# Projecting all keys and values in the prologue of a two-layer gated cross-attention kernel, with its loads and small steps put in another order

## The chip, the cores and the metric

The kernel runs on one core of a Trainium2 chip. The metric is device time in microseconds (us), the median of several executions. A separate profiled execution supplies the trace; its engines are PE (TensorE matmul), PEld (TensorE weight load), DVE (VectorE), ACT (ScalarE), POOL (GpSimd) and SP (SyncE, which here issues most transfers).

## What is computed

Two layers over x of 16 batches x 128 tokens x 256 channels. `ctx` has the same shape. Layer 0 is a WKV scan over `ctx` and a gated FFN; layer 1 is a cross-attention in which the 128 token positions are the channels (16 heads of 8), and a mixture of experts:

```python
x = x + tanh(g_xattn[0]) * wkv(time_decay, time_first, layernorm(x), ctx)      # scan along the tokens
x = x + tanh(g_ffn[0])   * ffn(layernorm(x))                                    # 256 -> 704 -> 256
# cross-attention, for each batch; target = layernorm(x), source = ctx
q = einsum('oc,bct->bot', Wq, target) + bq[None, :, None]
k = einsum('oc,bcs->bos', Wk, source) + bk[None, :, None]
v = einsum('oc,bcs->bos', Wv, source) + bv[None, :, None]
dot = einsum('bhdt,bhds->bhts', q, k) / sqrt(HEAD_DIM)
dot = mask * dot - (1.0 - mask) * NEG
out = einsum('bhts,bhds->bhdt', softmax(dot) * mask, v)
x = x + tanh(g_xattn[1]) * out
x = x + tanh(g_ffn[1]) * moe(layernorm(x))                                      # 8 experts of 256 tokens, 1 shared
```

The keys and values depend on `ctx`, `Wk`, `Wv`, `bk` and `bv` alone, not on x.

## The kernel before

Batches are taken in four groups (NG) of four (GB). The program has three blocks, one after the other. At the end of a block every engine waits for all the others, SP too.

**Block 1, the prologue (L497 to L759)**, holds WKV for all groups and the FFN for groups 0 to 2. SP issues the loads: x of group 0, the mask, `ctx` of group 0 into the one buffer `CV`, 15 small vectors (all counted on `s_ld`), the FFN weights (`s_wts`), then the next `ctx` once PE has read the last (`s_vT`), the other x, and the late weights. WKV of a group and half goes: PE turns the normalised x and `CV` (`pe_wkv_in`), ACT takes exponents (`act_exps`), DVE multiplies and scans (`dve_products`, `dve_scans`), POOL adds (`pool_sums`), DVE takes a reciprocal (`dve_recip`), POOL multiplies (`pool_quot`, writes Y), PE turns Y back (`pe_wkv_out`) and DVE adds it to X (`dve_x1`). After `dve_ln2` and `pe_z2T` comes the FFN of the group: six slices i, each with a gate and an up product on PE (`pe_gu`), a tanh on ACT, two steps on DVE (`dve_h1`, `dve_h`); slice i+2 reuses the banks of slice i and waits for its `dve_h`. `pe_down` follows. While group g is in the FFN, WKV of group g+1 runs in between, at places written by hand (`pe_group`, `dve_group`, `act_group`, `pool_group`).

In this block DVE also makes the mask rows `mparts` from `mrow` (L684 to L696 and three calls of `mask_part`, at L698, L716 and L720); the last call adds to `s_mp`. SP waits for `s_mp` at L547, issues 14 transfers of mask rows to the scratch tensor `stack_scr` in HBM (L567; 16 batches x 2 sides x 192 rows of 512 B, 3.1 MB), and waits at L569 until all have landed.

**Block 2, attention (L1224 to L1492)**. For each batch PE projects q from `Z3` and k from `CX` (`pe_proj_q`, `pe_proj_k`), ACT adds biases into `QK` (`act_qk`), POOL applies the mask (`pool_masked`), ACT and POOL split into bf16 parts, SP stores these to `stack_scr` and reads the stacked rows, with the mask rows, back into `QKA`. PE makes scores, DVE takes maxima (`dve_reduce`, 16 for each batch), PE makes turned scores, ACT takes exponents, PE multiplies with the values `VP`. Values: `pe_v` from `CX`, `dve_vf` adds the bias into `VF`, POOL writes `VP`. The order is a hand-written table of 8 slots p for each batch (`turns`). The block opens with the FFN of group 3, with the first projections and scores in between.

**Block 3, the experts (L1582 to the end)**, is not touched.

The engines do what is queued on them strictly in program order, so a wait holds all that stands behind it on that engine.

Of the kernel before, what the change touches and what calls it, by code (L numbers as in the profile page):

```python
# [50 lines left out]
def flamingo_kernel(nc, x, ctx, mask, g_xattn, g_ffn, time_decay, time_first, gate_wT, up_wT, down_wT,  # L51
# [10 lines left out]
    with ExitStack() as keep:  # L62
# [123 lines left out]
        with ExitStack() as part:  # L186
# [21 lines left out]
            CV = sbw("CV", [P, GB, C])  # L208
# [36 lines left out]
            s_c = semp("s_c")  # L245
# [5 lines left out]
            s_mT2 = semp("s_mT2")  # L251
            s_mask = semp("s_mask")
# [7 lines left out]
            s_xr = semp("s_xr")  # L260
            s_var2 = semp("s_var2")
# [22 lines left out]
            WB = [bank[4], bank[5]]  # L284
# [4 lines left out]
            def pe_wkv_in(pe, g, h):  # L289
# [4 lines left out]
                pe.wait_ge(s_exp, 2 * n)  # L294
# [3 lines left out]
                if h == 0:  # L298
                    pe.wait_ge(s_c, 16 * (g + 1))
                pe.wait_ge(s_pab, 2 * n)  # L300
                for b in range(GB):
                    last = pe.transpose(WB[1][:, b * P:(b + 1) * P], CV[:, b, h * P:(h + 1) * P], ident[:])
                last.then_inc(s_vT, 1)

            def act_exps(act, g, h):
# [6 lines left out]
            def dve_products(dve, g, h):  # L312
# [36 lines left out]
            def pe_wkv_out(pe, g):  # L349
# [9 lines left out]
            def dve_x1(dve, g):  # L359
# [11 lines left out]
            def dve_stats1(dve, ch, g):  # L371
                if isinstance(g, int) and g == 0:
                    dve.wait_ge(s_x, 16)
                else:
                    dve.wait_ge(s_xr, 16 * (NG - 1))
# [120 lines left out]
            N_SMALL, N_ROWS = 15, 14  # L496
            with nc.Block() as block:  # L497
                @block.sync
                def _(sp):
# [6 lines left out]
                    def load_ctx(g):  # L506
                        sp.dma_start(CV[:, :, :], ct[:, bass.ds(GB * g, GB), :]).then_inc(s_c, 16)

                    small = [(gates[:, 0:2], g_xattn.partition_broadcast(P)), (gates[:, 2:4], g_ffn.partition_broadcast(P)),
                             (td[:], time_decay), (tf[:], time_first),  # L510
                             (gs[:, 0:NI - 1], gate_s[0:(NI - 1) * P].rearrange("(i p) -> p i", p=P)),
                             (us[:, 0:NI - 1], up_s[0:(NI - 1) * P].rearrange("(i p) -> p i", p=P)),
                             *[(dst[HALF_I * f:HALF_I * (f + 1), NI - 1:NI], src[(NI - 1) * P:INTER].rearrange("(p a) -> p a", a=1))
                               for dst, src in ((gs, gate_s), (us, up_s)) for f in range(2)],
                             (dsb[:], down_s.partition_broadcast(P)), (bvb[:], bv.partition_broadcast(P)),
                             (bqk[:, 0:1], bq), (bqk[:, 1:2], bk), (wq[:], wqT)]
                    assert len(small) == N_SMALL
                    with nc.allow_non_contiguous_dma(reason="small vectors"):
                        load_x(0)
                        sp.dma_start(mrow[:], mask).then_inc(s_mask, 16)  # L520
                        load_ctx(0)
                        for dst, src in small:
                            sp.dma_start(dst, src).then_inc(s_ld, 16)
# [6 lines left out]
                    sp.wait_ge(s_vT, 1 + 2)  # L530
                    load_ctx(1)
                    for g in range(1, NG):
                        load_x(g, s_xr)
                    sp.wait_ge(s_pool0, 10)
                    for dst, src in ((wk[:], wkT), (wv[:], wvT),
                                     (wgt[:, :, 0:NE], Wg.rearrange("(h p) e -> p h e", p=P)),
# [5 lines left out]
                    with sp.Fori(2, NG) as g:  # L542
                        sp.wait_ge(s_vT, 1 + 2 * g)
                        load_ctx(g)
# [221 lines left out]
            with ExitStack() as att:  # L766
# [228 lines left out]
                def dve_vf(dve, b):  # L995
                    dve.wait_ge(a_vps, b + 1)
                    if later(b):
                        dve.wait_ge(a_vp, b)
# [999 lines left out]
```

## Time and profile before

| | us |
|---|---|
| median of 3 runs | 587.51 (583.6, 587.51, 588.49) |
| the profiled execution | 581.58 |
| its span, first to last instruction | 579.8 |
| block 1 | 0 to 149.2 |
| in it, the first FFN product of group 0 | 43.3 |
| block 2 | 149.2 to about 434 |
| block 3 | about 434 to 579.8 |

Busy shares of the span: PE 84%, DVE 69%, PEld 46%, ACT 42%, POOL 38%. The mean granted TensorE clock is 0.978 of full speed. HBM reads are 39.01 MB, writes 22.43 MB. A share is a mean over stages with different limits, so the stages are read one by one: who is idle, and what released it.

### The profile page before, as it was taken

How to read it: one execution, taken by the hardware profiler on the slowest of the kernel's cores; microseconds unless marked ns; L12 is line 12 of the kernel's file. 1: busy time of each engine (PE TensorE's matmuls, PEld its weight loads, DVE VectorE, ACT ScalarE, POOL GpSimd, SP SyncE). 2: the span in 40 equal slices, each digit the busy share in tenths (PEclk: the TensorE clock that was granted, in tenths of full speed). 3: DMA queues.
4: the chain of work that ended last, by engine and by line, in shares of the span. 5: the costliest groups of instructions: out<-in, count | busy, mean ns of one | idle time of the engine just before them, and what ended most of it. 6: DMA issues, size and time to landing. Idle time of an engine off the chain costs nothing. (4 is left out here: it accounts for less than half of the span.)

```text
span 579.8 us, 10728 instructions
## 1 busy us (share of the span) xinstructions
PE 487.7 (84%) x3400; PEld 269.2 (46%) x3400; DVE 397.8 (69%) x871; ACT 243.7 (42%) x478; POOL 217.8 (38%) x353
## 2 busy tenths in 40 slices
PE   1149999999696769899988888888779999899994
PEld 1034564747353424333343343333233555578883
DVE  4989879695336778888888888887755733333331
ACT  1132233121231048777777777777741001123331
POOL 2526234231283235555555555531301370024334
PEclk9999999999997969999999999999899999999998
DMA  5901007630267054655555555450004024157873
GB/s 139 334 2 36 1 6 119 88 43 0 73 179 191 20 135 131 154 157 145 140 154 144 144 145 144 125 128 5 5 2 149 32 105 138 55 126 194 195 151 36
DMA packets 68246, 61.94 MB, mean 107 GB/s; under 512 B 8992, under 2 KB 63248, under 8 KB 68208
## 3 DMA queue, kind: packets, MB, share of 16 engines
q1 hardware_dynamic: 65136, 57.25, 37.8%
q0 software_dynamic: 3072, 4.21, 4.3%
q8 instruction: 20, 0.33, 0.2%
q14 instruction: 18, 0.15, 0.1%
HBM read 39.01 MB, written 22.43 MB: 106 GB/s over the span
## 5 line engine op out<-in xcount | busy, mean ns | idle before, releaser
L1008 DVE TENSOR_REDUCE MX<-psum 128x2 f32<-128x512 f32 x256 | 166.3, 681 | 31.6 <-PE psum L874 31.5
L1086 ACT ACTIVATE HP<-psum 128x512 f32<-128x512 f32 x256 | 138.6, 600 | 43.6 <-PE psum L880 42.9
L874 PE MATMUL psum<-QKA 60*128 60x256 bf16 x512 | 82.0, 279 | 18.3 <-DVE MX L1008 16.7
L880 PE MATMUL psum<-QKA 60*128 60x256 bf16 x512 | 80.0, 277 | 9.4 <-ACT HP L1086 7.4
L953 PE MATMUL psum<-HP,VP 128*32 128x256 f32 x1024 | 82.9, 397 | 0.2 <-ACT HP L1086 0.2
L437 PE MATMUL psum<-space_a,space_w 128*128 128x512 f32 x160 | 72.8, 606 | 4.1 <-PEq L497 2.4
L874 PEld LDWEIGHTS psum<-QKA 60*128 60x128 bf16 x512 | 35.3, 95 | 64.9 <-DVE MX L1008 47.8
L1656 POOL DMA_INDIRECT out_x<-OE,to_u x16 | 25.0, 1562 | 72.6 <-ACT OE L1697 70.2
L437 PEld LDWEIGHTS psum<-space_a,space_w 128*128 128x128 f32 x160 | 29.8, 193 | 40.4 <-issue 34.4
L1795 PE MATMUL psum<-XT,WE 128*128 128x256 f32 (+1 forms) x192 | 44.1, 380 | 1.6 <-ACT XT L1681 1.6
L1721 PE MATMUL psum<-space_a,wsh 128*128 (+3 forms) x96 | 42.8, 595 | 0.8 <-PEq L1224 0.8
L880 PEld LDWEIGHTS psum<-QKA 60*128 60x128 bf16 x512 | 33.2, 95 | 20.7 <-ACT HP L1086 14.8
L478 PE MATMUL psum<-space_w,HP 128*128 128x256 f32 x160 | 41.2, 404 | 1.7 <-DVE HP L464 1.7
L1795 PEld LDWEIGHTS psum<-XT,WE 128*128 128x128 f32 (+1 forms) x192 | 34.2, 181 | 8.2 <-issue 1.1
L450 ACT ACTIVATE space_a<-psum,hgs 128x512 f32<-128x512 f32 (+1 forms) x24 | 15.5, 647 | 49.7 <-PE psum L437 38.8
L1116 POOL TENSOR_TENSOR VP<-VF,maskT 128x32 f32<-128x32 f32 x128 | 25.9, 239 | 26.9 <-DVE VF L999 15.8
L478 PEld LDWEIGHTS psum<-space_w,HP 128*128 128x128 f32 x160 | 30.2, 198 | 9.0 <-issue 5.5
L1098 POOL TENSOR_TENSOR QK<-QK,MB 128x512 f32<-128x512 f32 x16 | 20.3, 1269 | 36.0 <-ACT QK L1059 36.0
L953 PEld LDWEIGHTS psum<-HP,VP 128*32 128x32 f32 x1024 | 20.6, 109 | 26.9 <-issue 16.6
L1949 DVE SCALAR_TENSOR_TENSOR H1s<-THs,psum 128x256 f32<-128x256 f32 (+1 forms) x24 | 10.1, 420 | 31.5 <-ACT THs L1688 31.5
L334 POOL TENSOR_TENSOR DEN<-SB,EB 128x512 f32<-128x512 f32 x8 | 18.6, 2327 | 34.3 <-DVE SB L324 34.3
L1666 ACT ACTIVATE THs<-psum 128x512 f32<-128x512 f32 (+1 forms) x12 | 7.1, 595 | 55.0 <-PE psum L1721 55.0
(183 smaller groups left out, 739.8 us busy)
## 6 DMA issues: line engine op xcount, KB each, us to landing
QKA<-stack_scr SPq DMA_DIRECT2D x32, 480.0 KB, 5.4
stack_scr<-PARTS SPq DMA_DIRECT2D x32, 192.0 KB, 2.1
WE<-in_W SPq DMA_DIRECT2D x16, 352.0 KB, 4.0
stack_scr<-PARTS SPq DMA_DIRECT2D x32, 128.0 KB, 1.9
XD<-dispatched SPq DMA_DIRECT2D x8, 258.0 KB, 3.7
X<-in_x SPq DMA_DIRECT2D x4, 512.0 KB, 5.5
CV<-in_ctx SPq DMA_DIRECT2D x4, 512.0 KB, 3.6
CX<-in_ctx SPq DMA_DIRECT2D x16, 128.0 KB, 5.1
```

Of the source, the lines that this page charges most:

```text
L437: last = pe.matmul(to[:, :], w[:, h, i * P:(i + 1) * P], ZT[:, h, :], start=(h == 0), stop=(h == 1))
L478: pe.matmul(to[f], HP[:, i, t * P:(t + 1) * P], dw[:, i, :], start=(i == 0), stop=False)
L874: return pe.matmul(to[:, tt * T:(tt + 1) * T], QKA[rows, k, 0, h, tt * P:(tt + 1) * P], QKA[rows, k, 1, h, :], start=True, stop=True)
L880: return pe.matmul(to[:, (j % 2) * T:(j % 2 + 1) * T], QKA[rows, k, 1, h, st * P:(st + 1) * P], QKA[rows, k, 0, h, :], start=True, stop=True)
L953: last = pe.matmul(PVB[32 * j:32 * j + 32, grp * T:(grp + 1) * T], VP[:, k, st, 4 * j + i, :], PT[:, i % 2, st, j, :], start=(i in (0, 3) ...
L1008: dve.tensor_reduce(MX[:, par, head_of(n), :], src[:, :].rearrange("p (a s) -> p a s", a=2), axis=AX.X, op=ALU.max).then_inc(a_red, 1)
L1086: act.activation(PT[:, i % 2, st, 2 * half:2 * half + 2, :].rearrange("p j t -> p (j t)"), TBK3[THIRDS[m]], ACT.Exp).then_inc(a_exp, 1)
L1098: pool.tensor_tensor(QK2, QK2, MB[:, k, :].unsqueeze(1).broadcast_to([P, 2, T]), ALU.mult).then_inc(a_masked, 1)
L1116: last = pool.tensor_tensor(dst, src, maskT[:, st, bass.ds(b, 1)].unsqueeze(2) .broadcast_to([P, 4, 8]), ALU.mult)
L1656: pool.indirect_dma_start(out=out_rows, out_offset=bass.IndirectOffsetOnAxis(ap=to_u[:, e, a:a + 1], axis=0), in_=OE[:, s, a, :], in_offse ...
L1721: last = pe.matmul(bank[2 * i + side][0:m, :], (wsh1, wsh3)[side][:, h, i * P:i * P + m], ZT4[:, h, bass.ds(GT * g, GT)], start=(h == 0), ...
L1795: last = pe.matmul(bank[i][0:m, lo:lo + CAP], w[:, s, h, i * P:i * P + m], XT[:, s, h, :], start=(h == 0), stop=(h == 1))
```

## The change

All of `ctx` is loaded once, in block 1, into `CTX` (16 batches), and stays there for the block. PE projects keys and values of all 16 batches in 16 units (`pe_keys_values`: a unit is two batches' keys or two batches' values), 12 before `pe_wkv_out` of group 0 and 4 after; ACT copies them to `KR` (with the key bias) and `VR`, which live through block 2. In block 2 `pe_proj_k`, `pe_v`, `dve_vf`, the key half of `act_qk` and the `CX` loads are gone; POOL masks keys and queries in two steps and adds the value bias itself in `pool_vp`.

Block 1 is put in another order as well: five small vectors are loaded from ACT's queue and have a semaphore of their own (`s_chain`); the ten other small ones are issued behind the FFN weights; the multiplication of `dw` by `dsb` goes from DVE to POOL; group 0's second half uses two further banks (`WB2`); `dve_recip(g + 1, 0)` stands behind slice 0 instead of ahead of it; the making of the mask rows goes from the start of the block to the DVE work of the last group.

```diff
+            def pe_keys_values(pe, u):
+                j, side = divmod(u, 2)
+                if u == 0:
+                    pe.wait_ge(s_wkv, 32)
+                if side == 0 and j % 2 == 0:
+                    pe.wait_ge(s_c[j // 2], 16)
+                if u == 1:
+                    pe.wait_ge(s_mT2, 1)
+                if u >= 2:
+                    pe.wait_ge(s_keep, u - 1)
+                if side == 0:
+                    last = pe.matmul(KV[0][:, :], wk[:], CTX[:, 2 * j:2 * j + 2, :].rearrange("p b t -> p (b t)"),
+                                     start=True, stop=True)
+                else:
+                    for b in range(2):
+                        for st in range(2):
+                            last = pe.matmul(KV[1][:, (2 * b + st) * P:(2 * b + st + 1) * P],
+                                             CTX[:, 2 * j + b, st * P:(st + 1) * P], wv[:], start=True, stop=True)
+                last.then_inc(s_pr, 1)
...
                     for h in range(2):
                         pool_sums(pool, 0, h)
+                    pool.wait_ge(s_wts, 80)
+                    pool.wait_ge(s_ld, 16 * N_SMALL)
+                    pool.tensor_tensor(dw[:, :, :], dw[:, :, :], dsb[:, :].unsqueeze(1).broadcast_to([P, NI, C]),
+                                       ALU.mult).then_inc(s_dw, 1)
                     for h in range(2):
                         pool_quot(pool, 0, h)
...
-                    with pe.Fori(0, NG - 2) as g:
-                        pe_group(g, False)
-                    pe_group(NG - 2, True)
+                    for g in range(NG - 1):
+                        pe_group(g, g == NG - 2)
...
                     def dve_group(ch, g, last):
-                        dve_recip(dve, g + 1, 0)
                         for i in range(NI):
                             dve_h1(dve, ch, g, i)
                             dve_h(dve, ch, g, i)
                             if i == 0:
+                                dve_recip(dve, g + 1, 0)
                                 dve_products(dve, g + 1, 1)
                                 dve_scans(dve, g + 1, 1)
                             if i == 1 and not last:
                                 dve_stats1(dve, ch, g + 2)
+                            if i == 1 and last:
+                                mask_lines()
+                                mask_part(0)
                             if i == 2:
                                 dve_recip(dve, g + 1, 1)
+                            if i == 3 and last:
+                                mask_part(1)
                             if i == 4:
                                 dve_x1(dve, g + 1)
                         dve_ln2(dve, ch, g + 1)
                         if not last:
                             dve_products(dve, g + 2, 0)
                             dve_scans(dve, g + 2, 0)
+                        else:
+                            mask_part(2)
...
-                def pe_proj_k(pe, g, k):
-                    pe.wait_ge(a_cx[k], 32 * (g + 1))
-                    pe.matmul(MISC[:, T:2 * T], wk[:], CX[:, k, :], start=True, stop=True)
...
                 def pool_masked(pool, g, k):
-                    pool.wait_ge(a_qk, 2 * (GB * g + k) + 2)
-                    pool.wait_ge(a_cx[k], 32 * (g + 1))
-                    pool.tensor_tensor(QK2, QK2, MB[:, k, :].unsqueeze(1).broadcast_to([P, 2, T]), ALU.mult).then_inc(a_masked, 1)
+                    b = GB * g + k
+                    pool.wait_ge(a_cx[k], 16 * (g + 1))
+                    if later(b):
+                        pool.wait_ge(a_rest, 2 * b)
+                    pool.tensor_tensor(QK[:, T:2 * T], KR[:, bass.ds(b, 1), :].rearrange("p b t -> p (b t)"), MB[:, k, :], ALU.mult)
+                    pool.wait_ge(a_qk, b + 1)
+                    pool.tensor_tensor(QK[:, 0:T], QK[:, 0:T], MB[:, k, :], ALU.mult).then_inc(a_masked, 1)
...
-                def pool_vp(pool, g, k):
+                def pool_vp(pool, pch, g, k):
                     b = GB * g + k
-                    pool.wait_ge(a_vf, b + 1)
+                    pch.do(pool.tensor_tensor(VF[:, :, :], VR[:, bass.ds(b, 1), :, :].rearrange("p b s c -> p (b s) c"),
+                                              bvb[:, :].unsqueeze(1).broadcast_to([P, 2, P]), ALU.add))
+                    pch.wait()
```

What it moves on the engines, at three places. First DVE in the last group of block 1 of the changed kernel, from slice 2 to the end of the block (`mtmp` and `mparts` are the mask rows; `HP` is written by `dve_h`, the L140 to L128 rows by `dve_ln2`).

```order
L779 CAST mparts<-mtmp 16x3x256
L785 TENSOR_TENSOR mtmp<-mtmp,mparts 16x768
L503 SCALAR_TENSOR_TENSOR space_a<-space_a,psum 128x512
L512 SCALAR_TENSOR_TENSOR HP<-space_a,hgu,psum 128x512
L411 SCALAR_TENSOR_TENSOR X<-psum,tg,X 128x512 x2
L503 SCALAR_TENSOR_TENSOR space_a<-space_a,psum 128x256
L512 SCALAR_TENSOR_TENSOR HP<-space_a,hgu,psum 128x256
L122 BN_STATS stats<-X 128x6 x4
L126 BN_AGGR mv<-stats 128x2 x4
L128 TENSOR_SCALAR veps<-mv 128x4
L135 TENSOR_SCALAR space_a<-X,mv,rstd 128x256 x4
L779 CAST mparts<-mtmp 16x3x256
```

Before, DVE had in block 1, around the layer norm of group 0:

```order
L378 TENSOR_SCALAR negm<-mv 128x4
L363 SCALAR_TENSOR_TENSOR X<-psum,tg,X 128x512 x2
L122 BN_STATS stats<-X 128x6 x4
L126 BN_AGGR mv<-stats 128x2 x4
L128 TENSOR_SCALAR veps<-mv 128x4
L135 TENSOR_SCALAR space_a<-X,mv,rstd 128x256 x4
L690 CAST mparts<-mtmp 16x3x256
L318 TENSOR_TENSOR PA<-EA,psum 128x4x127
```

The last cast, which raises `s_mp`, stood behind the layer norm of group 0; now it stands behind that of group 3, near the end of the block.

Second, SP at the end of block 1 in the changed kernel: the 14 transfers of mask rows, and what stands ahead of and behind them.

```order
L591 DMA wsh<-in_sw 96x256
L612 DMA stack_scr<-mparts 16x48x256 [waits s_mp]
L612 DMA stack_scr<-mparts 16x32x256
L612 DMA stack_scr<-mparts 16x16x256 x4
L612 DMA stack_scr<-zeros 16x48x256
L612 DMA stack_scr<-mparts 16x16x256 x6
L612 DMA stack_scr<-onesb 16x96x256
L546 UNCONDITIONAL_BRANCH [waits s_mst]
L1267 UNCONDITIONAL_BRANCH [waits barrier_Pool_Activation_PE_DVE_SP_release]
L1186 DMA MB<-in_mask 128x256 x4
```

The same transfers stood here before, with the same two waits around them; what moved is the place on DVE at which `s_mp` is raised.

Third, POOL in block 1 of the changed kernel, between the sums of group 0 and its quotients (Y).

```order
L382 TENSOR_TENSOR DEN<-SB,EB 128x512
L384 TENSOR_TENSOR NUM<-SA,PB 128x512
L677 TENSOR_TENSOR space_w<-space_w,dsb 128x1536
L395 TENSOR_TENSOR Y<-NUM,DEN 128x512 x2
L437 TENSOR_TENSOR rstd<-veps,neghalf 128x4
```

The row L677 is new on POOL; it was on DVE, after group 0's last step.

## Rows read from the trace of the kernel before

**Rows 1.** By stage: stage, us, busy PE PEld DVE ACT POOL (x), PEclk, DMA share, GB/s.
```profile
0.00:43.30 43.30, 10.47 (x43) 8.02 (x43) 33.15 (x66) 8.78 (x16) 14.56 (x25) 1.00 0.50 159
43.30:149.20 105.90, 100.53 (x400) 59.32 (x400) 85.81 (x139) 24.97 (x42) 34.88 (x25) 1.00 0.26 40
149.20:209.50 60.30, 45.62 (x197) 23.51 (x197) 34.31 (x64) 11.90 (x23) 25.58 (x46) 0.92 0.45 121
209.50:434.00 224.50, 198.04 (x2220) 85.50 (x2221) 188.74 (x459) 168.53 (x335) 99.70 (x216) 0.98 0.46 117
```
**Rows 2.** What SP's queue waited for at the end of block 1: total us, times, longest.
```profile
SPq L497 <- PEq L497: 25.7, 1, 25.7
SPq L497 <- DMA stack_scr<-onesb: 11.7, 1, 11.7
```
**Rows 3.** SP's issues in order of time: start, us, line, transfer, count.
```profile
85.66 11.00 SPq L567 DMA_DIRECT2D stack_scr<-mparts  x6
...
110.16 1.46 SPq L567 DMA_DIRECT2D stack_scr<-onesb  x1
149.19 0.38 SPq L1143 DMA_DIRECT2D CX<-in_ctx  x1
```
**Rows 4.** Busy time by stretch, columns as in the first group: the opening loads, the mask stores.
```profile
20.00:30.00 10.00, 0.00 (x0) 0.00 (x0) 10.00 (x5) 0.00 (x0) 5.84 (x5) 1.00 0.91 307
...
90.00:95.00 5.00, 5.00 (x13) 2.07 (x12) 4.74 (x15) 1.37 (x2) 3.49 (x4) 1.00 0.68 88
```
**Rows 5.** DVE in order of time, block 1, with what ended its idle time.
```profile
9.45 0.68 DVE L686 TENSOR_SCALAR mtmp<-mrow 16x256 f32<-16x256 f32 x3
...
11.14 0.94 DVE L696 TENSOR_TENSOR mtmp<-mtmp,mparts 16x768 f32<-16x768 f32 x1
13.33 0.17 DVE L700 TENSOR_SCALAR upos<-tf 128x2 f32<-128x2 f32 x1 [1.24 <-DMA wq<-in_wqT]
...
15.27 0.68 DVE L318 TENSOR_TENSOR PA<-EA,psum 128x508 f32<-128x508 f32 x1 [0.49 <-ACT EA L310]
...
23.20 6.53 DVE L340 RECIPROCAL DEN<-DEN 128x512 f32<-128x512 f32 x2
...
33.91 1.40 DVE L363 SCALAR_TENSOR_TENSOR X<-psum,tg,X 128x512 f32<-128x512 f32 x2
...
81.86 3.34 DVE L340 RECIPROCAL DEN<-DEN 128x512 f32<-128x512 f32 x1
...
139.40 1.38 DVE L135 TENSOR_SCALAR space_a<-X,mv,rstd 128x256 f32<-128x256 f32 x4 [1.13 <-POOL rstd L146]
```
**Rows 6.** PE in order of time, block 1 and the opening of block 2.
```profile
31.12 1.97 PE L355 MATMUL psum<-ident,Y 128*128 128x128 f32 x8 [13.41 <-POOL Y L347]
...
99.50 1.09 PE L355 MATMUL psum<-ident,Y 128*128 128x128 f32 x8 [0.88 <-POOL Y L347]
...
153.31 0.70 PE L851 MATMUL psum<-CX,wk 128*128 128x256 f32 x2 [2.12 <-DMA MB<-in_mask]
```
**Rows 7.** POOL's additions of 512 elements: count, ns min/median/max.
```profile
L334 POOL TENSOR_TENSOR DEN<-SB,EB x8: 2092/2098/3916, 17.8 to 123.1; 128x512 f32<-128x512 f32 x8
L336 POOL TENSOR_TENSOR NUM<-SA,PB x8: 1257/1266/1279, 19.8 to 125.2; 128x512 f32<-128x512 f32 x8
```
**Rows 8.** PE, then DVE, in one batch of the attention loop.
```profile
305.12 0.71 PE L859 MATMUL psum<-wv,CX 128*128 128x128 f32 x4
305.76 0.28 PE L874 MATMUL psum<-QKA 60*128 60x256 bf16 x1
...
311.20 0.70 PE L855 MATMUL psum<-Z,wq 128*128 128x256 f32 x2 [0.42 <-DVE Z L993]
...
306.19 0.69 DVE L1008 TENSOR_REDUCE MX<-psum 128x2 f32<-128x512 f32 x1 [0.34 <-PE psum L874]
306.80 0.41 DVE L999 TENSOR_TENSOR VF<-psum,bvb 128x256 f32<-128x256 f32 x1
307.13 0.68 DVE L1008 TENSOR_REDUCE MX<-psum 128x2 f32<-128x512 f32 x1
```

More of the change, by code:

```diff
@@ L282, in flamingo_kernel, with later, pe_wkv_in @@
             s_x2 = primed("s_x2")
-            WB = [bank[4], bank[5]]
+            WB, WB2 = [bank[4], bank[5]], [bank[2], bank[3]]
             DB = [bank[6], bank[7]]
             after_wkv = []
-            def pe_wkv_in(pe, g, h):
+            def later(count):
+                return not isinstance(count, int) or count > 0
+            def pe_wkv_in(pe, g, h, WB=WB):
                 n = 2 * g + h
@@ L293, in pe_wkv_in @@
                     pe.wait_ge(s_x1, 2 * g)
-                pe.wait_ge(s_exp, 2 * n)
+                if later(n - 1):
+                    pe.wait_ge(s_exp, 2 * n)
                 for b in range(GB):
@@ L506, in load_ctx @@
                     def load_ctx(g):
[L507 to L523, printed above, removed]
+                        sp.dma_start(CTX[:, GB * g:GB * (g + 1), :], ct[:, GB * g:GB * (g + 1), :]).then_inc(s_c[g], 16)
+                    load_x(0)
+                    load_ctx(0)
+                    sp.dma_start(mrow[:], mask).then_inc(s_mask, 16)
+                    for dst, src in ((wk[:], wkT), (wv[:], wvT)):
+                        sp.dma_start(dst, src).then_inc(s_wkv, 16)
+                    load_ctx(1)
+                    load_ctx(2)
+                    load_x(1, s_xb)
+                    load_ctx(3)
                     sp.dma_start(gw[:, :, :], gate_wT.rearrange("(h p) i -> p h i", p=P)).then_inc(s_wts, 16)
@@ L572, in _ @@
                 def _(act):
-                    act.wait_ge(s_ld, 16 * N_SMALL)
+                    chain = [(td[:], time_decay), (tf[:], time_first),
+                             (gates[:, 0:2], g_xattn.partition_broadcast(P)), (gates[:, 2:4], g_ffn.partition_broadcast(P)),
+                             (bqk[:, 1:2], bk)]
+                    assert len(chain) == N_CHAIN
+                    with nc.allow_non_contiguous_dma(reason="small vectors"):
+                        for dst, src in chain:
+                            act.dma_start(dst, src).then_inc(s_chain, 16)
+                    act.wait_ge(s_chain, 16 * N_CHAIN)
                     act.activation(tg[:], gates[:], ACT.Tanh).then_inc(s_act0, 1)
```

228 lines of the change are left out of this document (108 added, 120 removed).

## Prediction

> **What bounds the kernel now.** I read the stages first, then who was released by whom at each stage's end. Four stages matter [rows 1]. Up to 43.3 us DVE is busy 33.2 of 43.3 us and PE 10.5: the first WKV group is a chain through DVE, ACT and POOL, and PE idles. From 43.3 to 149.2 PE is busy 100.5 of 105.9 us: three FFN groups, PE bound. The opening of attention, to 209.5, is a chain with no engine full. In the attention loop PE has 198.0 and DVE 188.7 of 224.5 us: both are nearly full, and each waits for the other in short pieces. The expert block behind it is untouched.
>
> The reader is to see one more thing, which no busy share shows. At the end of block 1 SP waited 11.7 us for the last mask store and then 25.7 us for the other engines [rows 2]. The stores went out from 85.66 us; the last was issued at 110.16, took 1.46 to issue and landed 11.7 later, at 123.3 [rows 3]. 123.3 + 25.7 = 149.0, and SP's next issue is at 149.19. So the block opens for all when the last has come, and the stores had 25.7 us to spare. They need 123.3 - 85.7 = 37.6 us, at a steady 88 GB/s with the transfer engines 0.68 busy [rows 4]: 3.1 MB at 88 GB/s is 36 us, which agrees.
>
> **The mask stores.** The change raises `s_mp`, for which they wait, behind the layer norm of group 3. That layer norm ended at 139.40 + 1.38 = 140.8 us before [rows 5]. When is it now? Three terms.
>
> Start of block 1. `upos` at 13.33 waited for `wq`, the last of 15 small loads [rows 5]. The five vectors of the chain now come on ACT's queue. Z1 of group 0 is ready at 9.5 (the mask lines follow it at 9.45), PE turns it with four transposes (half of the eight that took 1.97 after idling [rows 6], so 1.0 to 1.1), ACT takes two exponents of the size of DVE's product, 0.68 each [rows 5], and with the hand-overs the first product starts at about 12.1 instead of 15.27: 3.2 earlier. Both reciprocals end at 23.20 + 6.53 = 29.7 before, at 26.5 now. POOL, however, has the multiplication of `dw` by `dsb` ahead of Y. It waits for all weights and ten small loads behind 5.6 MB in SP's queue; at the 307 GB/s of a loaded stretch [rows 4] that is 18 us after a start near 3, so about 22, just when the sums are done (22.4). Its 1536 elements are not in the trace on POOL. Bounds: three times the 1.26 us of the NUM addition is 3.8, three times the median 2.10 of DEN is 6.3 [rows 7]. I take 3.8, because it runs beside DVE's reciprocal, as the second NUM did. Y is then ready at 22.4 + 3.8 + 2 x 1.26 = 28.8 instead of 31.1 [rows 6]. X was added at 33.91 to 35.3, because DVE was late [rows 5]; it ends at about 31.6 now, 3.7 earlier. The layer norm behind it moves along; `pe_wkv_in` of group 1 now stands between the turned layer norm and the first FFN product and takes back 0.3, so that product starts at 39.9 instead of 43.3. With POOL at 6.3 it is 2.5 less.
>
> The DEN addition took 2.1 us beside a scan and NUM 1.26 beside a reciprocal [rows 7]. The Trainium skill, SBUF — State Buffer, Who interferes with whom, has it that a DVE instruction with two SBUF inputs blocks a GpSimd one that reads SBUF, and one with a single input outside the two-port modes does not. By that rule 3.8 is right here and the 6.3 would need a scan beside it; the trace agrees with its two durations.
>
> The keys and values cost nothing there: eight units of keys (two batches, 512 columns) and eight of values. A value pair of one batch occupies PE for 0.64 us and a key projection for about 0.5 [rows 8], so a unit is 1.0 to 1.3, the 16 are 16 to 20 us. Their cover is PE's idle time, 13.4 us before Y in one piece [rows 6] and 32.8 of 43.3 in all [rows 1]. Without that cover they would cost these 16 to 20.
>
> DVE in the groups. In group 0 the products of group 1 now stand behind the layer norm, and `dve_recip` (3.3) behind slice 0. Worked through: scans to 44.4, slice 0 to 45.9, DEN to 47.1, reciprocal to 50.4, products and scans to 53.9, slice 1 to 55.3; PE could use its bank from 51.6 and waits. Two more slices, the statistics and the second reciprocal give Y of group 1 at 63.4, some 2.0 earlier than before, and that is what is left when group 1 begins. In groups 1 and 2 DVE used to take the reciprocal at 81.86 to 85.2, while PE made slice 0 [rows 5]; now it idles there about 1.2 us and takes it behind slice 0: +1.2 each.
>
> In group 2 DVE has the mask lines and two splits as well. The first piece took 9.45 to 12.08 [rows 5], 2.6 us; the second is a cast and a subtraction, 2 x 0.94 to 2.2. I count 4.8 less the slack of about 1 that PE leaves: +3.8. Then the last cast, 1.0.
>
> `s_mp` is raised at 140.8 - 2.0 + 1.2 + 1.2 + 3.8 + 1.0 = 146.0 us. The stores follow: 146.0 + 37.6 = 183.6, and 0.5 for the release. Block 2 opens at 184.1 instead of 149.2: **+34.9 us**. PE's own end, at about 152, lies under that and does not matter.
>
> A page prices them otherwise. The Trainium skill, DMA: Bandwidth & Descriptors, Measured (HBM→SBUF, 128 partitions, SWDGE, issued from GpSimd), gives 341 GB/s for 1 MB; by that 3.1 MB would be an estimated 9 us, and the sum below would come out some 28 lower. The row says 88 GB/s for these 512 B rows from 16 partitions, so the measurement decides.
>
> **The opening of attention.** PE waited 2.12 us for the first `CX` and `MB` [rows 6]; now q waits only for Z3, 0.9 earlier. Three value pairs and two key projections leave PE ahead of the first scores, five pieces which I put at 0.44 each, below the 0.64 of rows 8 since they overlap their neighbours there: 2.2. Together -3.1. After 35 us of idling PE is slow at first: eight transposes took 1.97 us after 13.4 idle, 1.09 in a busy stretch [rows 6]. Most of that falls before Z3 is ready: +0.5. Sum **-2.6**.
>
> **The loop.** Per batch, slot 6 loses the values on PE, 305.12 to 305.76, and slot 7 the bias on DVE, 306.80 to 307.13. DVE waited 0.34 for PE ahead of that [rows 8]. PE comes 0.64 earlier, DVE uses 0.34 of it and saves another 0.33: 0.67 a batch. The key projection gives nothing: q behind it waited 0.42 for Z3 anyway, Z3 hangs on DVE and POOL, so the wait grows by what the projection leaves. Bounds: 0.33, if only DVE's own time counts; 0.64 + 0.44 = 1.1, if PE's time does. Values are projected in 13 slots, the other three in the opening: 13 x 0.67 = **-8.7** (-4.3 to -14). POOL takes 256 more elements a batch (0.66) but is busy 99.7 of 224.5 us [rows 1], and the query half of its masking is ready earlier.
>
> **Sum.** 34.9 - 2.6 - 8.7 = +23.6 on 581.58, the profiled execution's own time: 605.2. The median of the three runs lies 5.9 above that execution. I add a little for it and say 606.
>
> **The rivals.**
> *The stores don't hold the block.* The other side. If block 2 could open when PE is done, at 152.6, then 3.4 - 2.6 - 8.7 = -7.9, 574 us. Against it: SP's wait at L569 is in the order unchanged, and rows 2 add up only if all wait for SP. Chance 0.02.
> *The stores are quicker when nothing runs beside them.* They decide from 37.6 - 23.6 = 14 us down, 225 GB/s; at that speed the kernel is as before, 582; at 307 GB/s, 10 us, it is 578. Against it: the rate was constant at 88 while DVE and PE were busy, and nothing else moved data. Chance 0.05, split.
> *The loop is PE bound.* Then -14 instead of -8.7, 600. PE's idle time in front of DVE speaks against it. 0.15.
> *The first scores after the long idle run at a low clock,* as the opening already shows in its mean of 0.92 [rows 1], and POOL's multiplication runs at 6.3: +5 to +10, 610 to 616. 0.13.
> *My forecast*, 0.65, with its own range 601 to 611.
>
> **How the numbers follow.** The range takes the forecast and the two cases on either side of it: from 600 less 4 for the start of block 1, to 616 plus the offset of the runs; 596 to 618. This kernel can tell about 1%, 6 us. Slower by over 1%: 0.93. Within 1%: 0.04, the quick stores near 14 us. Faster: 0.03.
>
> **What would show it.** Right: SP issues the first mask store at about 146 and all engines stand still until about 184; the expert block as long as before; the attention period shorter by 0.67 a batch. The start: `upos` at 9.5, Y near 28.8, the first FFN product near 40. Wrong: mask stores that land in under 20 us; a value bias on POOL that makes DVE wait; a period that hasn't changed, which would mean that PE's and DVE's waits merely grew.

## The result and the profile after

| | before | after |
|---|---|---|
| median, side by side | 586.49 us (583.6 to 588.49, 4 runs) | 622.6 us (622.25 to 623.27, 4 runs) |
| ratio | | 1.062, 95% interval 1.057 to 1.067 |
| profiled execution, its span | 581.58, 579.8 | 622.25, 620.5 |
| block 2 opens | 149.2 | 189.15 |
| mean granted TensorE clock | 0.978 | 0.941 |

The change makes the kernel 6.2% slower. The direction and the place were forecast; the time lies 4.6 us above the range's upper end. The medians differ by 36.1 us and the two profiled executions by 40.7: the profile before, at 581.58, is quicker than all four of its timed runs. The stages below are compared by these two profiles. By stage, the columns those of [rows 1]:

```profile
0.00:44.80 44.80, 24.88 (x123) 18.48 (x123) 29.02 (x56) 17.66 (x31) 17.87 (x26) 0.89 0.56 178
44.80:189.20 144.40, 101.44 (x402) 59.43 (x401) 91.46 (x148) 25.96 (x44) 33.05 (x25) 0.89 0.18 22
189.20:246.70 57.50, 43.25 (x177) 20.84 (x178) 34.20 (x61) 10.45 (x19) 28.33 (x53) 0.89 0.45 119
246.70:470.80 224.10, 180.92 (x2144) 74.00 (x2145) 191.40 (x446) 164.63 (x323) 110.53 (x242) 0.97 0.43 110
```

The second stage has PE busy for the same 101 us and is 38.5 us longer. In the loop PE does 17 us less than in [rows 1] and the loop is no shorter. What SP waited for around the end of block 1, and its issues, against [rows 2, 3]; then 24 us of it with the busy columns:

```profile
SPq L612 <- DVE mparts L779: 122.9, 1, 122.9
SPq L546 <- DMA stack_scr<-onesb: 11.5, 1, 11.5
...
SPq L546 <- PEq L546: 0.2, 1, 0.2
```

```profile
151.53 10.79 SPq L612 DMA_DIRECT2D stack_scr<-mparts  x6
...
175.83 1.46 SPq L612 DMA_DIRECT2D stack_scr<-onesb  x1
189.15 1.79 SPq L1186 DMA_DIRECT2D MB<-in_mask  x4
```

```profile
160.00:184.00 24.00, 0.00 (x0) 0.00 (x0) 0.00 (x0) 0.00 (x0) 0.00 (x0) 0.53 0.71 88
```

The 25.7 us in which SP waited for PE have become 0.2: now all wait for SP. In these 24 us no compute engine has an instruction, and the stores move 88 GB/s. From the first issue at 151.5 to the last landing (175.83 + 1.46 + 11.5 = 188.8) they take 37.3 us.

The 40.7 us by which the span grew, piece by piece. The loop is taken from 209.56 (246.7 after) to the last turn of `YA`, in which PE turns a batch's attention result back.

| | before | after | difference | forecast |
|---|---|---|---|---|
| until block 2 opens | 149.2 | 189.15 | +39.95 | +34.9 |
| opening of attention | 60.4 | 57.6 | -2.8 | -2.6 |
| loop | 223.1 | 222.8 | -0.4 | -8.7 |
| rest, mainly block 3 | 147.1 | 151.0 | +3.9 | 0 |

### The profile page after: what moved, and what is told of

The parts are those of the page before. It is cut to its first block and busy times, and to the rows that moved or that the text cites. A ratio compares the mean times of both kernels' runs of the same rounds, so it can differ in the third digit from the quotient of the medians.

```text
span 620.5 us, 10647 instructions
## 1 busy us (share of the span) xinstructions
PE 484.0 (78%) x3384; PEld 265.4 (43%) x3384; DVE 401.7 (65%) x854; ACT 248.3 (40%) x478; POOL 232.8 (38%) x386
## 5 line engine op out<-in xcount | busy, mean ns | idle before, releaser
L1047 DVE TENSOR_REDUCE MX<-psum 128x2 f32<-128x512 f32 x256 | 164.2, 679 | 30.9 <-PE psum L920 30.7
L485 PE MATMUL psum<-space_a,space_w 128*128 128x512 f32 x160 | 74.7, 618 | 39.2 <-PEq L546 32.4
L920 PEld LDWEIGHTS psum<-QKA 60*128 60x128 bf16 x512 | 34.5, 95 | 76.5 <-DVE MX L1047 54.5
L146 POOL TENSOR_TENSOR rstd<-veps,neghalf 128x1 f32<-128x1 f32 (+1 forms) x17 | 11.7, 689 | 91.4 <-DVE veps L128 65.8
L1815 PEld LDWEIGHTS psum<-XT,WE 128*128 128x128 f32 (+1 forms) x192 | 34.1, 181 | 10.3 <-DVE HE L1974 2.2
L926 PEld LDWEIGHTS psum<-QKA 60*128 60x128 bf16 x512 | 32.8, 95 | 13.1 <-ACT HP L1123 5.6
L122 DVE BATCH_NORM_STATS2 stats<-X 128x6 f32<-128x256 f32 (+1 forms) x36 | 12.5, 410 | 36.1 <-PEq L546 31.0
L1097 ACT ACTIVATE QK<-psum,bqk 128x256 f32<-128x256 f32 x16 | 7.6, 477 | 53.2 <-PE psum L907 51.8
```

The costliest lines, as they stand in the source:

```text
L485: last = pe.matmul(to[:, :], w[:, h, i * P:(i + 1) * P], ZT[:, h, :], start=(h == 0), stop=(h == 1))
L920: return pe.matmul(to[:, tt * T:(tt + 1) * T], QKA[rows, k, 0, h, tt * P:(tt + 1) * P], QKA[rows, k, 1, h, :], start=True, stop=True)
L926: return pe.matmul(to[:, (j % 2) * T:(j % 2 + 1) * T], QKA[rows, k, 1, h, st * P:(st + 1) * P], QKA[rows, k, 0, h, :], start=True, stop=True)
L1047: dve.tensor_reduce(MX[:, par, head_of(n), :], src[:, :].rearrange("p (a s) -> p a s", a=2), axis=AX.X, op=ALU.max).then_inc(a_red, 1)
L1815: last = pe.matmul(bank[i][0:m, lo:lo + CAP], w[:, s, h, i * P:i * P + m], XT[:, s, h, :], start=(h == 0), stop=(h == 1))
```

## The experiments

The second time beside each result is that of the kernel before on the same chip. Kernels measured on different chips are compared by their ratios to it.

**The mask stores.** Two kernels move the mask work: one moves it early again in the changed kernel, the other moves it late in the kernel before.

```diff
                     dve_stats1(dve, ch, 1)
+                    mask_lines()
+                    mask_part(0)
                     dve_x1(dve, 0, WB2)
...
+                    mask_part(1)
+                    mask_part(2)
                     dve_products(dve, 1, 0)
```

> The changed kernel with the mask work back in DVE's idle stretch of the first WKV group: mask lines and first split behind the second statistics, the other two splits ahead of the products of group 1. Nothing else changes, all of it is still computed. Theory (the stores hold block 2 shut): the stores now run under the FFN groups, block 2 opens when PE and the last layer norm are done, between 149 and 156 us instead of 189.2, and the time falls by 33 to 40, to 583 to 589 us. Rival (something else that the prologue now does holds the block, and the stores only lie beside it): block 2 still opens near 189, the time stays at 620 to 624.

Measured: 585.65 us against 584.17 before, ratio 1.004 (1.001 to 1.007). The changed kernel has 1.062, and 1.067 when measured again. SP's waits:

```profile
SPq L546 <- PEq L546: 70.5, 1, 70.5
SPq L612 <- DVE mparts L752: 17.5, 1, 17.5
```

The stores go out at 46.03 us and SP then has 70.5 us to spare. Block 2 opens at 153.99.

> The kernel before with one part of the change alone: its mask lines and splits are moved into the last group of block 1, where the changed kernel has them. Theory: the late start of the stores alone costs the loss: SP's first mask store at 140 to 147 us, block 2 opens some 37.5 later, at 178 to 185 instead of 149.2, and the time rises by 29 to 36, to 615 to 622 us. Rival (the values and keys in the prologue, or the bias, cost it): under 5 us more.

Measured: 617.22 against 584.17, ratio 1.056 (1.054 to 1.058). First store at 145.73, block 2 opens at 183.72, 34.5 later than in [rows 3]. So it is shown from both sides that the late start of the stores makes nearly all of the loss, and the projections in the prologue do not. What is left of it, 0.4% with early stores, is looked for below.

The second question is whether the 88 GB/s belong to SP's queue. Seven of the 14 stores were issued by ACT:

```diff
-                    for dst, src in rows:
+                    for dst, src in rows[0::2]:
...
+                    for dst, src in rows[1::2]:      # ACT
+                        act.dma_start(dst, src).then_inc(s_mst, 16)
```

> The changed kernel with every second of the 14 mask stores issued from ACT's queue, so that two queues work at the 3.1 MB at once. Theory (what bounds the stores is the transfer engines' handling of these 512 B rows from 16 partitions, 88 GB/s whatever issues them): from the first issue to the last landing still 36 to 38 us, the time within 2 us of 622. Rival (one queue's issue, 1.8 us a transfer and the packets behind it, is the bound): 19 to 26 us, the time 12 to 18 lower.

Measured: 620.45 against 583.87 before, ratio 1.063. Block 2 opens at 189.25, and the stretch from 160 to 184 reads the same as with one queue, 0.71 and 88. So the rate is not that of SP's queue. What in these transfers sets it (the 512 B rows, the 16 partitions, the writing to HBM) was not tried.

**The start of block 1.** `dw` times `dsb` is taken off POOL and put back on DVE:

```diff
-                    pool.wait_ge(s_wts, 80)
-                    pool.wait_ge(s_ld, 16 * N_SMALL)
-                    pool.tensor_tensor(dw[:, :, :], dw[:, :, :], dsb...)
...
                     dve.tensor_tensor(hgu[:], hgs[:], us[:], ALU.mult).then_inc(s_dv0, 1)
+                    dve.wait_ge(s_wts, 80)
+                    dve.tensor_tensor(dw[:, :, :], dw[:, :, :], dsb...)
```

> The changed kernel with the multiplication of dw by dsb back on DVE, behind hgu, so that GpSimd's Y does not stand behind a wait for all small loads and weights. Theory: Y of group 0 is ready at 27 to 29 us instead of 34.4, the first FFN product starts at 39 to 41 instead of 44.8, mparts is ready 3 to 6 us earlier, and the time falls by 3 to 6 us. Rival (the first group is held by DVE's own chain, its reciprocals and the later multiplication): the first FFN product stays within 1 us of 44.8 and the time within 1 us.

POOL in the changed kernel, then in this one:

```profile
21.58 1.26 POOL L384 TENSOR_TENSOR NUM<-SA,PB 128x512 f32<-128x512 f32 x1
28.52 3.42 POOL L677 TENSOR_TENSOR space_w<-space_w,dsb 128x1536 f32<-128x1536 f32 x1 [5.68 <-DMA wq<-in_wqT]
31.90 2.48 POOL L395 TENSOR_TENSOR Y<-NUM,DEN 128x512 f32<-128x512 f32 x2
```

```profile
23.89 1.27 POOL L395 TENSOR_TENSOR Y<-NUM,DEN 128x512 f32<-128x512 f32 x1 [1.03 <-DVE DEN L388]
27.10 1.26 POOL L395 TENSOR_TENSOR Y<-NUM,DEN 128x512 f32<-128x512 f32 x1 [1.95 <-DVE DEN L388]
```

POOL's multiplication waited 5.68 us for `wq`, the last of the small loads. Why did that one land at 28.5? SP's issues of the small loads in the changed kernel, then the same two `gs` in the kernel before, then the transfer engines in the changed kernel:

```profile
15.73 4.79 SPq L582 DMA_DIRECT2D gs<-in_gate_s  x2
...
23.43 0.43 SPq L582 DMA_DIRECT2D wq<-in_wqT  x1
```

```profile
5.59 1.27 SPq L523 DMA_DIRECT2D gs<-in_gate_s  x2
```

```profile
20.00:25.00 5.00, 5.00 (x28) 3.41 (x27) 5.00 (x3) 3.28 (x6) 2.84 (x2) 1.00 0.42 63
```

The large loads went as forecast: by 22 us 5.5 MB had moved (252 GB/s over these 22 us), and from 20 to 25 us the transfer engines were 0.42 busy. But SP issued the ten small loads only from 14.46 to 23.86, and `wq`, issued last, landed 5.0 us after its issue. While the large loads ran at up to 390 GB/s, the two `gs` took 4.79 us to issue instead of 1.27. So SP's issues behind the large loads came late, not the bytes; why those two took so long is not shown.

Without `dw` on POOL, Y is ready at 28.4 instead of 34.4, the first FFN product starts at 39.6 instead of 44.8, the first mask store at 146.37 and block 2 opens at 184.40. Time 614.59 against 584.17, 1.052 (1.049 to 1.055). The edit takes away the wait and the multiplication together; by the rows above, the wait is 5.68 of the 9.1 us.

The reciprocal of each group ahead of slice 0, as the kernel before has it, alone on the changed kernel:

```diff
+                        dve_recip(dve, g + 1, 0)
                         for i in range(NI):
...
                             if i == 0:
-                                dve_recip(dve, g + 1, 0)
                                 dve_products(dve, g + 1, 1)
```

> The changed kernel with one edit, DVE's first reciprocal of each group back ahead of slice 0. Theory (the forecast's +1.2 us in each of two groups and the later start of group 1's products): the first mask store at 147 to 149.5 us instead of 151.5 to 152.3, the time 2.5 to 4 us lower. Rival (the reciprocal only moves PE's waits, as the mask lines and splits in the last group set the end): the first mask store within 0.7 us of 151.9, the time within 1 us.

Measured: first store at 149.72, 1.8 and 2.6 earlier than in the two profiles of the changed kernel; 616.22 against 584.46, ratio 1.055 (1.050 to 1.060). The first store comes about 2.2 us earlier, for all three groups together, which is between theory and rival but nearer to the theory: PE's waits of 1.44 and 1.40 us for `HP` in groups 1 and 2 are gone. The rest of the time's gain is in the loop, 196.9 us from the first to the last turn of `YA` against 199.8, where one or two stretches at a low clock are missing. The kernel with two store queues, whose loop is that of the changed kernel, has 196.8 as well, so this part is put down to the execution and not to the edit.

**The loop: DVE against POOL.** One wait in `pool_masked` is moved back. It is the wait for ACT's biased query; the key half of the masking, which needs nothing from it, now stands behind it too, and all that follows on POOL comes later:

```diff
-                    pool.tensor_tensor(QK[:, T:2 * T], KR[:, bass.ds(b, 1), :]..., MB[:, k, :], ALU.mult)
                     pool.wait_ge(a_qk, b + 1)
+                    pool.tensor_tensor(QK[:, T:2 * T], KR[:, bass.ds(b, 1), :]..., MB[:, k, :], ALU.mult)
```

> The changed kernel with one wait moved: GpSimd's masking of the query half waits for the scores of both halves, as before the change, so that its addition of the rest comes later in a batch. Theory (DVE's L1066, 906 ns instead of 181, is stretched because GpSimd's addition of the rest now runs at the same time): L1066 is back below 300 ns, the period of a batch falls from 13.84 towards 13.4, and the time by 4 to 7 us. Rival one (the masking is then later by as much as DVE gains): L1066 is short, the period stays within 0.1 of 13.84. Rival two (L1066 is long for another reason, such as its operands' form): it stays at 0.9 us.

DVE and then POOL in a batch of the changed kernel:

```profile
339.44 0.97 DVE L1066 TENSOR_TENSOR RD<-RD,maskG 128x32 f32<-128x32 f32 x1
```

```profile
339.21 1.16 POOL L1144 TENSOR_TENSOR QK<-QK,PARTS 128x512 f32<-128x512 f32 x1 [0.82 <-ACT PARTS L1107]
```

All executions of L1066 (ns min/median/max), in the changed kernel, in the experiment, and of the same line in the kernel before:

```profile
L1066 DVE TENSOR_TENSOR RD<-RD,maskG x16: 181/906/972, 267.8 to 468.6; 128x32 f32<-128x32 f32 x16
```

```profile
L1066 DVE TENSOR_TENSOR RD<-RD,maskG x16: 180/181/193, 269.7 to 469.2; 128x32 f32<-128x32 f32 x16
```

```profile
L1027 DVE TENSOR_TENSOR RD<-RD,maskG x16: 179/181/191, 231.8 to 431.9; 128x32 f32<-128x32 f32 x16
```

A multiplication of 32 elements ends at 340.41, when POOL's ends at 340.37: it stood still behind it. The changed kernel had moved POOL's addition to this moment. The Trainium skill, SBUF — State Buffer, Who interferes with whom, states that a DVE instruction with two SBUF inputs and a GpSimd one that reads SBUF compete, and that the loser waits for the whole of the other. The trace agrees: 0.97 us instead of 0.18, ending with POOL's 1.16.

Batch by batch (a row: stretch between turns of `YA`, us; then the columns of [rows 1]). A steady one and the second before the end of the steady loop, first of the changed kernel, then of this experiment (its first batch as well), then of the kernel before:

```profile
327.68:341.53 13.85, 11.19 (x138) 4.66 (x138) 12.84 (x29) 10.61 (x22) 8.27 (x18) 1.00 0.55 142
...
422.45:437.24 14.79, 12.18 (x135) 4.60 (x135) 10.92 (x25) 9.38 (x19) 1.72 (x4) 0.88 0.14 31
```

```profile
271.46:289.54 18.08, 15.28 (x142) 5.66 (x138) 11.60 (x29) 11.12 (x23) 8.30 (x18) 0.72 0.56 133
...
330.17:343.37 13.20, 11.40 (x142) 4.84 (x138) 12.05 (x29) 10.48 (x23) 8.27 (x18) 1.00 0.59 149
...
421.43:437.76 16.33, 12.96 (x136) 4.87 (x136) 11.06 (x25) 9.50 (x19) 1.72 (x4) 0.79 0.20 45
```

```profile
346.02:360.08 14.06, 12.56 (x147) 5.48 (x144) 12.50 (x30) 10.97 (x24) 7.43 (x16) 1.00 0.58 150
...
386.24:399.37 13.13, 11.44 (x139) 4.91 (x139) 11.26 (x26) 9.25 (x19) 3.34 (x12) 1.00 0.17 36
```

At full clock the period is 14.06, 13.84 and 13.20: 0.64 us a batch are back. But from the first to the last turn of `YA` it is 199.1, 199.8 and 198.5 us, because two batches of the experiment take 18.1 and 16.3 us at a mean clock of 0.72 and 0.79. The time is 618.22 against 584.17, ratio 1.056 (1.052 to 1.061), an improvement on 1.062 and 1.067 that the intervals do not separate. The theory holds for the instruction and the period, not for the whole.

**The loop: the low clock.** In each low stretch the granted clock is 0.50, 1.2 GHz of 2.4, for about 3.4 to 10 us. The kernel before has one such stretch too, in the batch from 412.09 to 425.30 (mean 0.87, a little over 1 us longer), where no transfer is waited for. The first kernel here has the three edits (early mask work, `dw` on DVE, the joined masking); the second gives PE one more matmul a batch, whose result nobody reads:

```diff
                                 pe.wait_ge(a_nm, b + 2)
+                                pe.matmul(MISC[:, T:2 * T], wk[:], KR[:, k, :], start=True, stop=True)
                                 pe_proj_q(pe, *at(g, k, AHEAD_Q))
```

> Three edits at once on the changed kernel: the mask work back in the first group, the multiplication of dw back on DVE, GpSimd's masking of the query half behind the scores of both halves again. Theory (three causes that do not touch each other): against the changed kernel 34 less by the stores' start, 5 to 6 by the first group, and 4 to 9 by the loop (period 13.2 instead of 13.84, less what a low clock takes back): block 2 opens at 147 to 150 us, the time is 571 to 580 us, 1 to 2% below before. Rival one (the mask work in the first group costs what the move of dw gains): block 2 opens at 153 to 155, 578 to 583. Rival two (the low clock takes all of the loop's gain back, as in the run with the masking alone): first to last turn of YA 198 to 200 us, 580 to 583.

> The same three edits, and one matmul a batch whose result nothing reads (256 columns, the size of the key projection that the change took out) ahead of the projection of q, where PE otherwise waits for Z3. Theory (PE's granted clock falls in the loop where PE has had more idle time than before the change): at most one stretch of the loop is left at the low clock where the kernel without the extra matmul has two or three, and the time is 2 to 5 us lower. Rival one (the clock falls at a wait of 1.5 to 2 us for the stacked rows, whatever PE did before): the same stretches are slow, the time is the same or up to 3 us more. Rival two (the extra matmul stands on the path): period longer by 0.3 to 0.5, 4 to 7 us more.

Measured: 581.42 and 579.68 against 583.87, ratios 0.994 (0.991 to 0.998) and 0.992 (0.990 to 0.995). The first misses its range: block 2 opens at 152.85 (nearly rival one) and `YA` to `YA` takes 197.6 (nearly rival two). The extra matmul was to leave at most one low stretch; its profile has four batches below 0.95 instead of two, and 200.1 us from `YA` to `YA`. Both profiles are among the slowest executions of their kernels. Over ten executions each, the mean granted clock is 0.958 and 0.959, and the 1.7 us between the medians are within the intervals. So no help of the extra matmul is shown. What did PE do before the clock fell? In the second kernel:

```profile
321.29 0.28 PE L923 MATMUL psum<-QKA 60*128 60x256 bf16 x1 [1.95 <-DMA QKA<-max_scr]
```

So the next kernels send the maxima ahead of the 480 KB of stacked rows that they queued behind:

```diff
-                            if there(b, 3):
-                                sp_fill(sp, *at(g, k, 3))
                             if there(b, 1):
                                 sp_max_store(sp, *at(g, k, 1))
...
                                 sp_max_fill(sp, *at(g, k, 1))
+                            if there(b, 3):
+                                sp_fill(sp, *at(g, k, 3))
```

> The kernel with the three edits, and SP's order in the loop changed: the maxima of a batch are stored and read back ahead of the 480 KB of stacked rows of a later batch, not behind them. Theory (the low clock in the loop is started by PE's waits of 1.3 to 2 us for QKA from max_scr, which queue behind those 480 KB): SP's wait for max_scr, 4.0 to 4.6 us a batch, falls below 3, PE has no wait over 0.7 us for QKA from max_scr, the stretches at a mean clock below 0.95 go except those near the end of the loop, first to last turn of YA 190 to 194 us instead of 197.6, time 574 to 578. Rival one (the clock falls from PE's idle time as such): waits gone, stretches still there, 197 to 199. Rival two (the stacked rows then come late): PE waits for QKA from stack_scr and the loop is over 200 us.

> The kernel before with SP's order alone changed, the maxima ahead of the stacked rows. Theory (at its period of 14.06 us the kernel before hardly waits for the maxima, one wait of 0.67 us in the loop): the time stays within 0.4% of before. Rival (its loop, too, is set by SP's chain of transfers): 3 us or more lower.

Measured: 587.67 and 592.47 against 586.88, ratios 1.002 (0.999 to 1.005) and 1.007 (1.003 to 1.010). That is rival two of the first, though at 198.7 us from `YA` to `YA` and not over 200, and neither theory nor rival of the second, which lost 0.7% (205.8 us from `YA` to `YA`). SP's wait for `max_scr` fell from 63.9 to 10.2 us in the loop and PE no longer waits for it, but the stacked rows now come late. In the first of the two kernels, PE, and the batches with and without such a wait:

```profile
309.31 0.39 PE L917 MATMUL psum<-QKA 60*128 60x256 bf16 x1 [2.18 <-DMA QKA<-stack_scr]
```

```profile
303.90:320.80 16.90, 12.81 (x142) 5.11 (x138) 12.22 (x29) 10.61 (x23) 8.30 (x18) 0.90 0.60 152
320.80:334.00 13.20, 11.39 (x141) 4.76 (x137) 12.05 (x29) 10.41 (x23) 8.27 (x18) 1.00 0.49 132
...
387.44:400.54 13.10, 10.63 (x135) 4.40 (x135) 10.92 (x25) 9.29 (x19) 1.72 (x4) 1.00 0.26 69
```

The same batch that takes 16.3 us at 0.79 takes 13.1 at 1.00 when PE's longest wait in it is 1.25 us. A last kernel changes the order for batch 12 alone, on the best kernel so far (below), with that one beside it:

> The kernel with the four edits (mask work early, dw on DVE, query half of the masking behind both halves, reciprocal ahead of slice 0), and SP's order changed for batch 12 alone, the last for which stacked rows are still to be fetched: its maxima go ahead of them. Theory (the wait of 2 us for the maxima there starts the low clock that makes the second batch before the end of the steady loop 16.3 us long, and nothing soon needs the stacked rows): this batch takes 13.0 to 13.2 us at a mean clock of 1.00, the time is 2.5 to 3.5 us below the kernel without it. Rival (the clock falls there for another reason, such as the query projections that end with this batch): it takes 16 us again, the time is the same within 1 us.

> The kernel with the four edits once more, beside the one with SP's order changed for batch 12. Theory: 0.981 to 0.990 of before, 2.5 to 3.5 us above its neighbour, and the second batch before the end of the steady loop at 16.3 us with a mean clock of 0.79. Rival: as its neighbour within 1 us.

Measured: 576.47 and 578.09 against 584.46, ratios 0.986 (0.983 to 0.990) and 0.989 (0.985 to 0.994). The batch takes 15.10 us at 0.89 against 16.94 at 0.80: a wait of 1.96 for the stacked rows replaces 0.88 and 2.01. Half of the effect; the difference of the medians, 1.6 us, is within the intervals. Waiting is tied to the low clock in all of these, but no single wait decides: a wait of 1.15 in the kernel before, at 391.3, left it at 1.00, and in the changed kernel it fell at 301 after waits of 0.70 and 0.84 for DVE. Nor does it belong to the changed loop alone. The batch at the end of the steady loop ran at the full clock in the kernel with two store queues (the changed loop), and at a low one in the kernel before with late mask work (the loop of before), where PE had waited 2.37 us for the maxima:

```profile
421.54:434.42 12.88, 10.76 (x135) 4.38 (x136) 10.93 (x25) 9.30 (x19) 1.72 (x4) 1.00 0.13 26
```

```profile
421.21:436.57 15.36, 12.77 (x140) 5.13 (x140) 11.30 (x26) 9.47 (x19) 3.34 (x12) 0.89 0.19 42
```

**The better kernel.** The three edits, and the reciprocal ahead of slice 0:

> The kernel with the three edits (mask work early, dw on DVE, GpSimd's query half behind both halves), and DVE's first reciprocal of each group put back ahead of slice 0, where the kernel before has it. Theory (each group loses about 1.2 us by the reciprocal behind slice 0, and the first of them more): PE's waits for HP in block 1, 3.00, 1.44 and 1.40 us without this edit, fall to 1.1 or less, block 2 opens at 148.5 to 151 instead of 152.85, and the time is 3 to 4 us lower, 577 to 579. Rival (the reciprocal ahead of slice 0 makes PE wait as long there): block 2 opens within 0.7 of 152.85.

> Both edits, the reciprocal ahead of slice 0 and the maxima ahead of the stacked rows, on the kernel with the three. Theory: the two gains add, 571 to 576 us, 1.5 to 2% below before. Rival: only one of them is there, 576 to 579.

Measured: 578.53 and 585.23 against 586.88; 0.985 (0.981 to 0.990) and 0.997 (0.995 to 0.999). Block 2 opens at 148.81 instead of 152.85. So the rest of the change pays once the mask stores, `dw`, the reciprocal and the masking are put right: 1.1 to 1.5% faster, twice measured. By the profiles the gain is in block 2, where the projections are gone: 2.8 us from its opening to the first turn of `YA` (81.5 for 84.4) and 3.4 from there to the last (195.7 for 199.1), with block 1 as long as before. The projections were not tried apart from the rest of the new order. The gains of the two edits do not add, as the second one isn't a gain.

**Block 3.** It was 3.9 us longer without a change to its code.

> The changed kernel itself once more, beside the others on one chip. Its first profile has 11.2 us ahead of 517.6 us in which DVE and ACT wait for something that is none of the core's engines, and PE waits 1.6 us behind them. Theory (a stall of that one execution): it is gone, and block 3, from the last turn of YA to the end, takes 148.5 to 149.5 instead of 151.0; the time is 620 to 623 all the same, since the other executions are as long. Rival (the stall belongs to the program, by its layout or its instruction fetches): it is there again at the same instructions, block 3 takes 150.5 to 151.5.

Measured: 621.53 against 583.87, ratio 1.067 (1.060 to 1.073), and 147.6 us from the last turn of `YA` to the end, against 147.1 before and under the 148.5 to 149.5 expected. The stall is gone. In the first profile of the changed kernel DVE had:

```profile
517.69 0.75 DVE L1954 SCALAR_TENSOR_TENSOR X<-psum,tg,X 128x512 f32 x1 [7.04 <-remote]
```

The chain of the end holds 11.2 us "another core or an unknown queue" there. It came back in four more profiles, all from one chip, one of them of the kernel before with only SP's order changed; the other twelve profiles have none. So it is not of this change; what it is stays open.

## Why the prediction was right or wrong

- **The stores hold the block: right.** 37.6 us forecast, 37.3 measured, at the same 88 GB/s, with one queue or two.
- **When they start: 5.5 us late**, 151.5 instead of 146.0. The step that failed is the landing of the small loads, "about 22", taken from the bytes ahead of them at the 307 GB/s of [rows 4]. The bytes had moved by 22, but the ten issues and the way of the last one to its landing were put at nothing: it was issued at 23.43 and landed at 28.5, and two issues among them took 4.79 us instead of 1.27. POOL's multiplication itself was well sized, 3.42 for 3.8, though it ran beside the statistics of DVE and not beside a reciprocal. So Y came at 34.4 instead of 28.8 and the first FFN product at 44.8 instead of 39.9, 4.9 of the 5.5. With `dw` on DVE the store starts at 146.37 and the block opens at 184.40, for 146.0 and 184.1 in the sum.
- **DVE's groups: nearly.** From the first FFN product to the first store it took 106.7 us for 106.1. The reciprocal's place was priced 2.4 for groups 1 and 2 and measured about 2.2 for all three. The other terms (-2.0, +3.8, +1.0) were not measured one by one, so errors in them may have cancelled.
- **The opening: right**, -2.8 for -2.6. Q's first projection starts 4.2 us after block 2 opens instead of 4.7, as the sum had it (0.9 less 0.5). (In block 1, `upos` came at 10.3 instead of 9.5.)
- **The loop: wrong by 8.3**, and the largest error. The step that failed is "POOL takes 256 more elements a batch (0.66) but is busy 99.7 of 224.5 us [rows 1], and the query half of its masking is ready earlier". This was taken to be harmless. It moved POOL's addition onto DVE's 32 elements and cost 0.64 us a batch. Without that the period is 13.20, better than the 13.40 of the forecast. The other part is what keeps the 13.20 from shortening the loop: the waits for transfers and the low stretches, 1.4 to 4 us each. That the faster loop meets its transfers late is argued, not shown. Batch against batch of the two profiles, seven steady ones gave 1.8, the first three lost 2.2 and the batch at 422 lost 1.7, while a low stretch of the kernel before, at 412, gave 1.1 back; the first turn of `YA` was reached 1.0 earlier, and one batch gave 0.3. Whether the batch at 422 is slow differs between executions, and the medians grew 4.6 us less than the two profiles, so the 8.3 may be some us less for a typical execution; the steady period, 13.84 for 13.40, does not depend on that.
- **Block 3, 0: right** in the second profile (+0.5); the 3.9 of the first is a stall that other kernels have too.
- **The rivals.** A PE-bound loop (600) did not come: PE had 17 us less work and the loop kept its length. The low clock was priced for the opening alone (+0.5, or +5 to +10 by the rival). There the first four FFN products took 3.39 us instead of 1.96 and no more was lost; it came back in the loop.

The range was also put together wrongly: "616 plus the offset of the runs", with the 5.9 us that the prediction names, is 622 and not 618, and even that is short of the 622.6 measured. It should have reached to the case in which the loop gives nothing and the small loads are late, 605.2 + 8.7 + 5 = 619 for one execution, and more for a median.

## What to carry to other kernels

Before a producer is moved off "idle" time, look at what its result starts: here stores from 16 partitions that take 37 us, from one queue or from two. When small loads are moved behind large ones, count their issues on the queue and not only the bytes ahead of them. When an instruction is made ready earlier, ask which neighbour it now runs beside; a 0.18 us instruction can take five times as long. And a gain in a loop that nearly waits for its transfers must first be shown against that chain: here added waits of PE often, though not always, went with a low clock.

## What the hardware showed that was not expected

- DVE's single-source `veps` of 4 elements took 3.14 us beside POOL's multiplication of 1536 elements, both ending at 31.9 to 32.0; 10 us later the same line took 0.17.

```profile
28.82 3.14 DVE L128 TENSOR_SCALAR veps<-mv 128x4 f32<-128x4 f32 x1
```

- The 3.1 MB of mask rows go at 88 GB/s with the transfer engines 0.71 busy, the same from one queue and from two, with all else idle or with PE and DVE busy ([rows 4]: 0.68 and 88).
- The granted clock fell to 0.50 in the middle of a loop in which PE is busy 11 to 12 of 13 us, around waits of 0.7 to 2.4 us, and one such stretch made a batch 1.4 to 4 us longer.
